# A fused window-attention kernel: variances as four 64x64 products, and a new order of the blocks on every engine

## The reference

```python
# layer 0, windows of 4 x 4 pixels (16 tokens), 4 heads of 16
qkv = xw @ qkv_w.T + qkv_b
qn, kn = q / norm(q), k / norm(k)
attn = softmax(qn @ kn.T * scale + bias + mask)
out = (attn @ v) @ proj_w.T + proj_b
x = x + layernorm(out, norm1_g, norm1_b)
h = gelu(x @ fc1_w.T + fc1_b) @ fc2_w.T + fc2_b
x = x + layernorm(h, norm2_g, norm2_b)
# layer 1, on x seen as sequences of 256
trend = moving_average(x, 25)
xf = rfft(x - trend)[:, :128]
x = trend + irfft(einsum('bmnc,cmk->bknc', xf, w_real + 1j * w_imag))
```

## Time and profile before

| what | us |
| --- | --- |
| median of 3 runs | 8857.75 |
| lowest, highest | 8851.5, 8859.13 |
| profiled execution, its own time | 8850.95 |
| its span in the profile | 8849.2 |
| mean granted TensorE clock, share of full speed | 0.967 |
| busy TensorE | 8401.3 |
| busy ScalarE | 6230.1 |
| busy VectorE | 5742.6 |
| busy GpSimd | 5155.6 |

### The profile page before, as it was taken

The page is one execution under the profiler, slowest core; times in us unless marked ns, Lnnn a source line. Parts: engine busy times, 40 slices in busy tenths (PEclk is TensorE's granted clock), DMA queues, the critical chain, the costliest instruction groups (busy, mean ns, idle before and its releaser), DMA issues.

```text
span 8849.2 us, 652880 instructions
## 1 busy us (share of the span) xinstructions
PE 8401.3 (95%) x291636; PEld 5471.0 (62%) x291636; DVE 5742.6 (65%) x8029; ACT 6230.1 (70%) x8530; POOL 5155.6 (58%) x5127
## 2 busy tenths in 40 slices
PE   8799999999999999999999999999999999878686
PEld 5556666666666666666666666666666666557565
DVE  1457777777777777777777777777777777222121
ACT  1468888888888888888888888888888888322121
POOL 0357777777777777777777777777777777100000
PEclk9789999999999999999999999999999999889888
DMA  3111111111111111111111111111111111699999
GB/s 99 39 32 38 37 38 38 38 38 37 38 38 38 38 38 37 38 37 35 36 38 37 38 38 38 38 37 38 38 38 38 37 37 36 202 324 319 337 317 332
DMA packets 1105192, 700.01 MB, mean 79 GB/s; under 512 B 616850, under 2 KB 1026834, under 8 KB 1100948
## 3 DMA queue, kind: packets, MB, share of 16 engines
q1 hardware_dynamic: 1100484, 564.33, 23.9%
q10 hardware_dynamic: 4608, 134.22, 3.5%
HBM read 412.97 MB, written 285.21 MB: 79 GB/s over the span
## 4 chain that ended last, share of the span: by engine, by line
PE 93%; DMA 4%; issue 1%; SPq 0%; POOL 0%; DVE 0%; ACTq 0%; ACT 0%; POOLq 0%; DVEq 0%
PE ps L475 15%; PE ps L453 13%; PE ps L511 12%; PE ps L523 11%; PE ps L436 10%; PE ps L551 10%; PE ps L501 6%; PE ps L487 5%; PE ps L495 5%; PE ps L424 3%; DMA out<-arena 3%; PE ps L398 1%; PE ps L389 1%; PE ps L390 1%; SPq L262 0%
## 5 line engine op out<-in xcount | busy, mean ns | idle before, releaser
L475 PEld LDWEIGHTS ps<-arena 32*32 32x32 f32 x131072 | 1290.9, 104 | 541.8 <-issue 508.4
L475 PE MATMUL ps<-arena 32*32 32x16 f32 x131072 | 1425.4, 186 | 17.9 <-issue 12.6
L664 ACT ACTIVATE arena<-ps,arena 128x1024 f32<-128x1024 f32 x1024 | 1140.4, 1114 | 357.8 <-PE ps L523 205.9
L775 DVE TENSOR_TENSOR arena<-ps,arena 128x768 f32<-128x768 f32 x1024 | 962.1, 940 | 539.3 <-PE ps L436 539.3
L913 POOL TENSOR_TENSOR arena<-arena 128x512 f32<-128x512 f32 x512 | 536.9, 1049 | 1282.9 <-DVE arena L846 1009.9
L453 PEld LDWEIGHTS ps<-arena 32*32 32x32 f32 x131072 | 1167.1, 105 | 152.6 <-issue 152.6
L453 PE MATMUL ps<-arena 32*32 32x16 f32 x131072 | 1218.9, 180 | 34.3 <-issue 34.3
L960 POOL TENSOR_TENSOR arena<-arena 128x512 f32<-128x512 f32 x512 | 629.5, 1230 | 1037.6 <-DVE arena L827 1037.6
L551 PE MATMUL ps<-xch,amat 128*128 128x256 f32 x4096 | 924.6, 388 | 288.0 <-ACT arena L688 214.3
L511 PE MATMUL ps<-arena 64*128 64x512 f32 x4096 | 1178.9, 652 | 8.6 <-ACT arena L664 4.5
L922 POOL TENSOR_TENSOR arena<-arena 128x512 f32<-128x512 f32 x1024 | 1044.0, 1041 | 10.5 <-PE ps L475 10.4
(11 more groups left out here) (89 smaller groups left out, 14021.8 us busy)
## 6 DMA issues: line engine op xcount, KB each, us to landing
arena<-in_x SPq DMA_DIRECT2D x4096, 32.0 KB
y<-ystripe SPq DMA_DIRECT2D x256, 512.0 KB, 5.3
amat<-mix SPq DMA_DIRECT2D x512, 256.0 KB, 3.4
xch<-y SPq DMA_DIRECT2D x512, 256.0 KB, 4.0
out<-arena ACTq DMA_DIRECT2D x32, 4096.0 KB, 27.1
mix<-amat SPq DMA_DIRECT2D x64, 256.0 KB, 2.0
wri<-in_w_real SPq DMA_DIRECT2D x64, 64.0 KB, 1.8
wri<-in_w_imag SPq DMA_DIRECT2D x64, 64.0 KB, 1.9
```

The costliest lines, as they stand in the source:

```text
L475: ins = mm(PV[32 * h:32 * h + 32, b, c0:c0 + N], vexp[r, sl, h, :, :], pT[r, sl, h // 2, h % 2, :], start=True, stop=True, tile_position=( ...
L664: f(hT[kk], M, ACT.Gelu, bias=b1[:, kk:kk + 1]).then_inc(done, 1)
L775: tt(qkv[ring(g, 4)][:, :, 4 * pp:4 * pp + 4, :].rearrange("p w s n -> p s w n"), M.rearrange("p a (s n) -> p (a s) n", s=2)[:, :, 0:3 * C ...
```

## The change

The two variances of a step (first layernorm of group `i4`, second of `i6`) become one block, `variances`, of four 64x64 products. To give each its own quadrant of the array, the first layernorm's squares are taken with their halves crossed (`sq1x`): two DMAs of 128 KB on the sync engine's queue copy `sq1` there (`swap_halves`), for each group. The product from partitions 64 to 127 then writes partitions 0 to 63 and the other way round. Both variances have one semaphore.

qkv and the first layer no longer share one pair of banks: banks 0 and 1 (`MA`) take qkv and the first layer's second half, banks 2 and 3 (`MB`) its first half, the transposes of x and the variances. The scores and the weighted sums share banks 4 and 5, 256 columns each.

The order of the blocks is new on all engines. On TensorE the two halves of the first layer stand at the head of the step, scores come in two halves, one before the projection and one before the second layer, and the halves of the weighted sums stand on both sides of the variances and the second half of qkv. The weighted sums are now of group `i3` in the numbering of TensorE's step, the first layer of `i6`.

```diff
-        M = ps[:, 0:2, :]
-        S = ps[:, 2, :]
-        PV = ps[:, 3:5, 0:256]
-        PA = ps[:, 3, :]
-        D1, H2, TR = ps[:, 5, :], ps[:, 6, :], ps[:, 7, :]
-        XT, V1, V2 = D1, TR, PA
-
+        MA, MB = ps[:, 0:2, :], ps[:, 2:4, :]
+        PV = ps[:, 4:6, 0:256]
+        D1, H2 = ps[:, 6, :], ps[:, 7, :]
+        VV = MB
+        V1, V2 = VV[:, 0, :], VV[:, 1, :]
+        XT = MB[:, 0, :]
+
+        def S(sl):
+            return ps[:, 4 + sl // 4, 256:512]
+
+        def SC(sl):
+            return sl % 4 * 64
+
+        SR = ps[:, 4:6, 256:512].rearrange("p b (s n) -> p b s n", n=64)
...
+        def need_var(eng, h):
+
+            if there(h):
+                eng.wait_ge(var_ps, h.base + (h.off + 3))
+
...
-            for s, g in users:
-                if there(g):
+            for s, g, *h in users:
+                if there(g) or h and there(h[0]):
                     need(eng, s, g)
+                    if h:
+                        need(eng, l2_sb, h[0])
                     return
 
...
+            def swap_halves(g):
+                if there(g):
+                    need(sp, sq1_sb, g)
+                    for a in range(2):
+                        sp.dma_start(sq1x[a * C:a * C + C, :], sq1[(1 - a) * C:(2 - a) * C, :]).then_inc(sq1x_in, 16)
...
                     load_x(d * 2 + k // GPS, k % GPS, Group(d * 8, k))
+                    swap_halves(Group(d * 8, k - SWAP))
...
-                        after(pe, (dn1_sb, i5), (xT_sb, before(g)))
+                        after(pe, (gelu0, i6), (l1_sb, i5, i7), (xT_sb, before(g)))
...
-                            after(pe, (gelu0, i5), (gelu1, i6), (qkvB_sb, i1), (qkvA_sb, before(g)))
+                            after(pe, (gelu1, i6), (qkvB_sb, i1), (qkvA_sb, before(g)))
                         else:
-                            after(pe, (qkvA_sb, i0), (gelu0, i5), (gelu1, i6), (qkvB_sb, before(g)))
+                            after(pe, (qkvA_sb, i0), (gelu1, i6), (qkvB_sb, before(g)))
...
-                            need(pe, biased, before(g))
+                            after(pe, (oT_sb, i4), (biased, before(g)))
...
-                            after(pe, (l2_sb, i7), (oT_sb, before(g)))
+                            after(pe, (biased, i2), (oT_sb, before(g)))
...
-                        after(pe, (xT_sb, i0), (dn1_sb, before(g)))
+                        need(pe, dn1_sb, before(g))
...
+                def variances(g, h):
+                    if there(g) or there(h):
+                        need(pe, sq1x_in, g, 32)
+                        need(pe, sq2_sb, h)
+                        after(pe, (xT_sb, i0), (gelu0, i6), (l1_sb, before(g), before(h)))
+                        settled(pe)
+                        if there(g):
+                            for a in range(2):
+                                b = 1 - a
+                                ins = mm(V1[b * C:b * C + C, :], ones[a * C:a * C + C, a * C:a * C + C],
+                                         sq1x[a * C:a * C + C, :], start=True, stop=True, tile_position=(a * C, b * C))
+                        if there(h):
+                            for a in range(2):
+                                ins = mm(V2[a * C:a * C + C, :], ones[a * C:a * C + C, a * C:a * C + C],
+                                         sq2[a * C:a * C + C, :], start=True, stop=True, tile_position=(a * C, a * C))
+                        ins.then_inc(var_ps, 1)
...
-                            after(pe, (gelu1, i6), (qkvB_sb, i1), (qkvA_sb, i1), (gelu0, before(g)))
+                            after(pe, (l1_sb, i5, i7), (xT_sb, i1), (gelu0, before(g)))
                         else:
-                            after(pe, (qkvB_sb, i0), (qkvA_sb, i0), (gelu0, i5), (gelu1, before(g)))
+                            after(pe, (qkvB_sb, i1), (qkvA_sb, i1), (gelu1, before(g)))
...
+                first_layer(i6, 0, MB, fc1a_ps)
+                first_layer(i6, 1, MA, fc1b_ps)
+                scores(i2, 0)
+                project(i4)
                 turn_x(i0)
-                weighted(i4, 0, pvA_ps)
-                first_layer(i5, 0, fc1a_ps)
-                weighted(i4, 1, pvB_ps)
+                scores(i2, 1)
                 second_layer(i6, 0, fc2a_ps)
                 second_layer(i6, 1, fc2b_ps)
-                project(i4)
-                project_qkv(i0, 0, qkvA_ps)
-                variance2(i6)
-                variance1(i4)
-                project_qkv(i0, 1, qkvB_ps)
-                scores(i2, 0)
-                scores(i2, 1)
-                first_layer(i5, 1, fc1b_ps)
+                project_qkv(i0, 0, MA, qkvA_ps)
+                weighted(i3, 0, pvA_ps)
+                variances(i4, i6)
+                project_qkv(i0, 1, MA, qkvB_ps)
+                weighted(i3, 1, pvB_ps)
...
                 act.preload_act_table_set(EXP_SET)
-                exponent(i4)
+                log_norm(i2)
+                square2(i7)
+                root_norm(i2)
+                exponent(i3)
                 log1(i5)
-                log_norm(i2)
+                log2(i7)
                 root1(i5)
-                log2(i7)
-                root_norm(i2)
                 root2(i7)
                 act.preload_act_table_set(GELU_SET)
-                gelu(i6, 1, fc1b_ps, fc2b_ps, gelu1)
+                keep_o(i4)
+                gelu(i6, 0, MB, fc1a_ps, fc2a_ps, gelu0)
+                square(i1)
+                square1(i4)
+                gelu(i6, 1, MA, fc1b_ps, fc2b_ps, gelu1)
                 keep_x(i0)
-                square(i1)
-                keep_o(i4)
-                gelu(i5, 0, fc1a_ps, fc2a_ps, gelu0)
-                square2(i6)
-                square1(i4)
...
+                        need(dve, x1_sb, before(g))
...
+                sum_prob(i3)
+                turn_k(i2)
+                qkv_out(i1, 1, MA, qkvB_ps, qkvB_sb)
                 turn_q(i2)
+                normed1(i5)
+                normed2(i7)
+                invert(i3)
+                add1(i5)
                 sum_squares(i1)
-                turn_k(i2)
+                bias(i2)
+                turn_prob(i3)
                 clamp(i1)
-                qkv_out(i0, 0, qkvA_ps, qkvA_sb)
-                sum_prob(i3)
-                invert(i3)
-                qkv_out(i0, 1, qkvB_ps, qkvB_sb)
-                normed1(i4)
-                turn_prob(i3)
-                normed2(i6)
-                add1(i4)
-                bias(i2)
                 maximum(i2)
-                gain2(i6)
+                gain2(i7)
+                qkv_out(i0, 0, MA, qkvA_ps, qkvA_sb)
...
-                add_o2(i5)
-                expand_v(i3)
-                divide(i3)
-                norm_k(i1)
+                divide(i2)
                 add_o1(i0)
-                scale_norm(i1)
-                norm_q(i1)
+                add_o2(i4)
+                shift(i1)
+                scale_norm(i0)
+                norm_k(i0)
+                norm_q(i0)
+                expand_v(i1)
                 add2(i6)
-                shift(i2)
```

49 lines of the change are left out of this document (22 added, 27 removed).

## The result

| what | before, us | after, us |
| --- | --- | --- |
| median of 4 runs each | 8854.62 | 8729.6 |
| lowest, highest | 8851.23, 8859.13 | 8728.4, 8738.4 |
| span of the profiled execution | 8849.2 | 8728.2 |
| unrolled part ends (loop begins) | 558.6 | 530.5 |
| from there to the last turn's start | 6935.0 | 6857.2 |

The ratio is 0.9863, 95% interval 0.9851 to 0.9874: 1.4% faster. 8740 was forecast. Of the 121 us between the two spans 78 come from the loop, 28 from the unrolled part in front of it and 15 from behind it. The forecast had 114, 0 and 0.

The account below looks back on a forecast made before the run. TensorE's list of work was taken to bound the step: product changes cut 13.99 us to 13.11, control adds 0.65, giving 13.76. The 0.23 saved over 496 steps is 114 us, forecast 8740 us, range 8560 to 8960.

Parts of the forecast that it names:

- The bound: Window loop: a step lasts as long as TensorE's list of work, 13.99 us, so TensorE time saved counts fully.
- variances: TensorE's two variance blocks: 1.92 us becomes one stream of four 64x64 tiles, 1.06, minus 0.86 per step.
- weighted sums apart: TensorE's two weighted-sum blocks: if closeness makes one slow, spreading wins 0.10 us per step, bounds 0 and 0.25.
- loop control: TensorE's loop end behind small-tile weighted sums: 0.7 us of control minus 0.2 lead leaves 0.5 idle per step.
- register work before the variances: TensorE behind the weighted sums' first half: register work, wait and increment cost 0.15 us per step, bounds 0 to 0.3.
- I count no gain there: The 16 unrolled groups in front of the loop and 7 steps at the end: no gain from the new order.
- ScalarE's chain: Logarithms, exponentials, table load, weighted-sums copy: next scores would wait 0.4 us if control cost nothing; larger counts, not the sum.
- Rival (a): TensorE's loop control is hidden; step 13.5 us with ScalarE's 0.4, giving 8608 us; chance 0.13.
- Rival (b): The variances' quadrants don't run side by side; step 14.62 us, giving 9163 us; chance 0.12.
- Rival (c): Control or the squares' copy costs more than bounded; step 14.1 to 14.2 us, 8905 to 8960 us; chance 0.12.
- (d): All small terms cancel in the loop, step within 0.03 us of before; chance 0.06.
- One sign: ScalarE and VectorE busy shares of a loop stretch rise by 13.99/13.76, 2%.

Follow-up runs that it names:

- e2: Changed kernel with both first-layer halves at the step's end and ScalarE's copy of the weighted sums ahead of its second table load; 8556.46 us.
- e1: Changed kernel with both first-layer halves moved from the head to the end of TensorE's step, same sequence of blocks; 8751.14 us.
- e3: Changed kernel with both variances on the two diagonal quadrants, reading uncrossed squares, without the two copies per group; 9105.91 us.
- e6: Changed kernel without the two copies per group, the crossed product reading uncrossed squares; 8719.6 us.
- e10: Changed kernel with ScalarE's copy of the weighted sums ahead of its second table load, and two steps per turn of TensorE's loop; 12311.83 us.

## Why the prediction was right, and where not

**The bound** held: TensorE's list sets the step, and no engine became a new bound in after.

**Products.** Each term against the measured one, per step (before: the earlier trace rows and the mean of the steps from 3000 to 6000 us; after: the same):

| term | forecast | measured |
| --- | --- | --- |
| variances | -0.86 | -0.90 (1.92 to 1.02) |
| first layer in one piece | -0.20 | -0.19 (2.12 to 1.93) |
| projection and second layer apart | +0.16 | +0.15 (1.01 + 1.87 against 2.73) |
| scores in two blocks | +0.12 | +0.14 (mean 2.44 against 2.30) |
| weighted sums apart | -0.10 | +0.01 (mean 2.63 to 2.64, net of the two rows below) |
| loop control | +0.50 | +0.48 |
| register work before the variances | +0.15 | +0.15 (0.17 in the step shown) |
| sum | -0.23 | -0.16 |

**The term that failed** is "weighted sums: I take 0.10". I had read the difference of 1.19 and 1.39 in one step as the cost of closeness. Spread out, the two take 1.51 - 0.17 and 1.83 - 0.48 net of control, 1.34 and 1.35, in this step: they became alike, but not less in sum. That is 0.11 of the 0.23; the other terms are off by 0.04 together, the other way. So the loop gave 78 us, not 114.

**The steps outside the loop** also failed: "I count no gain there". The unrolled part gave 28 us and the part behind the loop 15. In the latter the channel stage itself is unchanged: from its first product to its last it takes 1197.5 us before and 1197.1 after. So the 15 lie in the last turn and the unrolled steps behind it, up to the channel stage's first product (115.8 to 101.1 us, at a granted clock of 0.76 and 0.85). The two errors, 36 too much and 43 too little, cancelled. The way and the main terms were right; that the total came so close was luck.

**Control** held in size, place and cause: a gap of 0.41 that names no data, with the branch inside, and gone in e2 when the block in front is a wide one. The Trainium skill's queue of 64 ("TensorE: Matmul & The Clock Gate", "Architectural detail: the array is 16× 32×32, not 1× 128×128") would have hidden most of it by the prediction's estimate of 0.5; the lead seen is 0.27. But that estimate had one load and one product for each small matmul, where the profile has two of each (128 loads and 128 products in a block of 1.19 us). By these records a lead of 64 instructions is 0.30 us, an estimate from the page's figure, and near the 0.27 of the trace; that the queue counts as the records do is not shown.

**ScalarE's chain** at "0.4, if control cost nothing" was 0.42 in e1. ScalarE's timeline of after shows that it ended shortly ahead of the need:

```profile
4011.33 0.69 ACT L665 ACTIVATE arena<-ps,arena 128x512 f32<-128x512 f32 x1 [0.98 <-PE ps L530]
...
4013.65 1.28 ACT L705 ACT_TABLE_LOAD   x1
4014.94 0.61 ACT L653 ACTIVATE arena<-ps 128x512 f32<-128x512 f32 x1
```

The copy ends at 4015.55, the next scores start 1.92 after 4013.88, at 4015.80: 0.25 of slack, less what waking costs (0.15 in e1, from the copy's end at 4010.20 to the scores at 4010.35).

**Rival (a)**, control hidden, was priced at 8608; e1 hid it and came to 8751. That price kept the 13.11 for the products, with its 0.10 for the weighted sums, and left out the 0.15 before the variances. The step came out 0.37 longer than 13.5; another 0.12 are the scores, whose two blocks take 2.54 in the mean in e1, where 2.30 and the 0.12 for the split would be 2.42. **Rival (b)**, quadrants in turn at 9163, is e3: 9106. **Rival (c)** shows in neither half: control cost 0.48, no wait of TensorE in after names the copies, and without them (e6) only 10 to 21 us go. **(d)** fell with the result. One sign came in half: the busy share of VectorE rose (759 to 785 us of 1000), that of ScalarE fell (824 to 817), and why it fell was not traced.

## What to carry to other kernels

Before an order is judged by its products, look at what stands behind the last block of a loop: behind a wide block its control is free, behind small tiles it cost 0.48 us a step here. When undoing one suspect changes nothing, look for a second one of the same length beside it, and take both away together. And a block that is split for one engine may be what gives another one its time: moving the scores' halves together cost 310 to 440 us, in good part through waits for ScalarE.

## What the runs showed of the hardware

- A loop body of two steps of this kernel made TensorE's branch 4.3 us long instead of 0.208, and the kernel 39% slower.
- Four 64x64 float32 products of 512 columns run together in 1.02 us with their change of shape, also where two write one bank in different partitions; on two quadrants in turn they take 1.90.
- `divide` on GpSimd takes 1.67 us in the new order against 1.23 (L960 before), `shift` 1.40 against 1.23, and VectorE's `add1` 1.37 against 0.75, with equal shapes. In one step `add1` runs from 4002.35 and `divide` from 4003.04, side by side; before, they were apart. In e10, whose steps are not all alike, `add1` takes 0.75 in each of the 250 steps in which nothing runs on GpSimd beside it, and 1.55 in the mean of the other 262, which GpSimd's work overlaps by 0.6 us or more. So its own slowness goes with GpSimd's work beside it; what makes `divide` and `shift` longer is open. It costs nothing on TensorE's path: from 3000 to 6000 us of after no wait of TensorE names VectorE or GpSimd.
